# Attention layer: inverting the softmax denominators on 32 partitions, and subtracting the mean through the weights

## The reference

```python
Q, K, V = (split_heads(x_flat @ W + b) for W, b in ((Wq, bq), (Wk, bk), (Wv, bv)))   # 4 heads of 32
attn = softmax(einsum('bhnd,bhmd->bhnm', Q, K) * scale, axis=-1)
out = einsum('bhnm,bhmd->bhnd', attn, V).transpose(0, 2, 1, 3).reshape(B, H * W, C)
y = out @ Wo + bo + x_flat
mu = mean(y, axis=-1)                       # over the 128 channels
var = mean(square(y - mu), axis=-1)
y = (y - mu) / sqrt(var + 1e-5) * gamma + beta
```

## Time and profile before

| What | Value |
|---|---|
| median of three runs | 5654.49 us |
| the profiled execution | 5656.6 us, span 5654.8 us |
| PE, DVE busy | 5338.5 us (94%), 4949.7 us (88%) |
| POOL, ACT busy | 4692.7 us (83%), 3876.3 us (69%) |
| first exp tile of slot 0, last finish's z stored (first layer) | about 94 us to 3768 us |
| mean DMA rate | 97 GB/s |

### The profile page before, as it was taken

The page is one execution under the profiler, slowest core; times in us unless marked ns, Lnnn a source line. Parts: engine busy times, 40 slices in busy tenths (PEclk is TensorE's granted clock), DMA queues, the critical chain, the costliest instruction groups (busy, mean ns, idle before and its releaser), DMA issues. The chain is left out here.

```text
span 5654.8 us, 81519 instructions
## 1 busy us (share of the span) xinstructions
PE 5338.5 (94%) x25264; PEld 2432.7 (43%) x25264; DVE 4949.7 (88%) x7220; ACT 3876.3 (69%) x7513; POOL 4692.7 (83%) x3661
## 2 busy tenths in 40 slices
PE   7999999999999999999999999968888888888888
PEld 3444444444444444444444444423333333333333
DVE  6888888888888888888888888829999999999998
ACT  3666666666666766666666666657777777777776
POOL 4888887888888788888788888747888888888887
PEclk8999999999999999999999999989999999999999
DMA  4111122211111211112211010225555555555555
GB/s 139 36 53 50 37 61 71 60 55 38 46 49 64 79 39 53 45 40 62 64 54 33 18 32 21 67 84 196 186 190 188 188 187 189 186 188 190 186 188 174
DMA packets 337475, 549.14 MB, mean 97 GB/s; under 512 B 76016, under 2 KB 99568, under 8 KB 335600
## 3 DMA queue, kind: packets, MB, share of 16 engines
q1 hardware_dynamic: 327536, 526.62, 28.8%
q10 hardware_dynamic: 9504, 17.31, 1.1%
HBM read 415.10 MB, written 109.84 MB: 93 GB/s over the span
## 5 line engine op out<-in xcount | busy, mean ns | idle before, releaser
L649 DVE TENSOR_REDUCE mpart<-ps 128x1 f32<-128x512 f32 x4096 | 2539.1, 682 | 536.4 <-PE ps L406 535.8
L533 ACT ACTIVATE exps<-ps 128x512 f32<-128x512 f32 x4096 | 2146.8, 600 | 1139.8 <-PE ps L413 1114.1
L406 PE MATMUL ps<-k_st,q_ring 96*128 96x512 f32 x4096 | 1778.2, 435 | 20.2 <-DMA k_st<-qk_split 15.6
L413 PE MATMUL ps<-q_ring,k_st 98*128 98x512 f32 x4096 | 1621.5, 397 | 3.8 <-ACT exps L533 3.4
L1300 POOL TENSOR_TENSOR hc<-hh,c_rep 128x512 f32<-128x512 f32 x1024 | 1295.8, 1278 | 310.8 <-DVE hh L1269 291.8
L1269 DVE TENSOR_TENSOR_SCAN hh<-d_a,carry,ps 128x512 f32<-128x512 f32 x1024 | 1311.9, 1284 | 0.0
L622 POOL TENSOR_TENSOR held<-exps 128x512 f32<-128x512 f32 x768 | 987.7, 1311 | 359.9 <-ACT exps L533 359.9
L406 PEld LDWEIGHTS ps<-k_st,q_ring 96*128 96x128 f32 x4096 | 774.7, 189 | 1136.5 <-DVE mpart L649 685.2
L622 POOL TENSOR_TENSOR sums<-exps 128x512 f32<-128x512 f32 x896 | 1134.5, 1282 | 72.0 <-ACT exps L533 70.0
L424 PE MATMUL ps<-exps,v_ring 128*32 128x512 f32 x8192 | 1092.4, 605 | 0.0
L413 PEld LDWEIGHTS ps<-q_ring,k_st 98*128 98x128 f32 x4096 | 778.3, 190 | 139.7 <-ACT exps L533 18.0
(11 more groups left out here) (113 smaller groups left out, 3881.3 us busy)
## 6 DMA issues: line engine op xcount, KB each, us to landing
d_a<-dt_dram SPq DMA_DIRECT2D x1040, 256.0 KB
qk_split<-hilo SPq DMA_DIRECT2D x128, 256.0 KB, 2.3
out_dram<-out_sb SPq DMA_DIRECT2D x128, 256.0 KB, 2.0
heads_in<-out_dram SPq DMA_DIRECT2D x32, 1024.0 KB, 5.2
q_ring<-qk_split SPq DMA_DIRECT2D x384, 64.0 KB, 2.0
k_st<-qk_split SPq DMA_DIRECT2D x45, 512.0 KB, 7.4
dt_dram<-dt SPq DMA_DIRECT2D x33, 512.0 KB, 5.5
s_u<-lo_u ACTq DMA_DIRECT2D x66, 256.0 KB, 5.9
```

The lines of the kernel that those rows point to most:

```text
L406: nc.tensor.matmul(d_bank(("max", m, t)), q_ring[0:PARTS, m % 4, 128 * i:128 * i + 128], k_st[0:PARTS, g % 2, chunk(kc)], start=True, stop ...
L413: nc.tensor.matmul(a_bank(("exp", n, t)), k_st[0:SHIFT, n // NCH % 2, 128 * t:128 * t + 128], q_ring[0:SHIFT, n % 4, :], start=True, stop= ...
L533: nc.scalar.activation(exps[:, u % EXPS, CH * half:CH * half + CH], a_bank(("exp", n, t)), ACT.Exp, scale=SCALE).then_inc(a_done, 1)
L649: nc.vector.tensor_reduce(mpart[:, m % 2, t % 4, t // 4:t // 4 + 1], d_bank(("max", m, t)), AX.X, ALU.max).then_inc(d_done, 1)
```

## The change

Four things, all in the first layer.

- **Denominators.** The parts of each head (4 rows of 512) go to DRAM, cut into 8 pieces of 64 columns, and come back as 32 partitions (head, piece) by 4 by 64 (`load_den`). DVE sums the four and takes the reciprocal (`invert`, step 4). SP stores the 32 by 64 reciprocals, waits for that to land, and loads them with each head's row repeated on its 32 partitions into `recip` (`spread_rec`). The product `spread_den`, and Ln and Exp on ACT, are gone.
- **Mean.** Once, in slot 6, DVE subtracts from each row of Wo its mean over output channels, and from bo its mean (`centre_weights`), so that the projection's result has mean zero. The mean of x over channels comes from a column of 1/128 beside Wv: the V projection has 129 columns, its extra one goes through `mean_st` to DRAM (one more store a projection), and each finish loads it back repeated on 128 partitions (`mean_x`). DVE makes x + bo - mean in step 1 (`centre_x`); `centre` adds it to the projection. The product with 1/128 and `add_x` are gone.
- **V in two parts.** 4 times 129 columns do not fit in one bank, so V takes two entries of DVE's ring, of three and one blocks, with two DVE operations each.
- **Order.** The join moves from step 5 to 6, normalisation from 5 to 6, the output projection from 6 to 7.

Left out of the diff below: setup loads and declarations, the removed functions `spread_den`, `mean`, `reciprocal` and `add_x` with their calls, which stand in the listing above, and what only renames.

```diff
--- before.py
+++ after.py
                 if v == 6:
-                    add(d, ("value", p))
+                    add(d, ("value", p, 0))
+                    add(d, ("value", p, 1))
             if g is not None and v == 1:
                 add(a, ("var", g))
             if f is not None:
-                if v == 4:
-                    add(a, ("den", f))
+                if v == 7:
+                    add(d, ("wo", f))
                 if v == 6:
-                    add(d, ("wo", f))
-                if v == 7:
-                    add(d, ("mean", f))
-                if v == 5:
                     add(d, ("join", f))
...
     out_dram = nc.dram_tensor("out_dram", [2, HEADS, 128, L], F32, kind="Internal").ap()
+    den_dram = nc.dram_tensor("den_dram", [2, NCH, HEADS, 8, 4, CH // 8], F32, kind="Internal").ap()
+    rec_dram = nc.dram_tensor("rec_dram", [HEADS, CH], F32, kind="Internal").ap()
+    mean_dram = nc.dram_tensor("mean_dram", [NF, CH], F32, kind="Internal").ap()
...
+        den_in = sb("den_in", [32, 4, CH // 8])
+        den = sb("den", [32, CH // 8])
+        rec = sb("rec", [32, CH // 8])
+        mean_st = sb("mean_st", [128, 4])
+        mean_x = sb("mean_x", [128, CH])
...
-                    sp.wait_ge(d_done, d_at["value", p] + 1)
+                    sp.wait_ge(d_done, d_at["value", p, 1] + 1)
+                    sp.dma_start(mean_dram[p, :].rearrange("(q j) -> q j", j=4), mean_st[:, :]).then_inc(mean_stored, 16)
                     sp.dma_start(v_dram[b, :, :, 128 * c:128 * c + 128].rearrange("h p x -> p h x"),
                                  v_stage[:, :, :, :].rearrange("p h t d -> p h (t d)")).then_inc(v_stored, 16)
...
                 def store_den(n):
                     f = batch_of(n) * NCH + n % NCH
-                    row, half = den_rows(f)
-                    row += 4 * (n // NCH % HEADS)
                     sp.wait_ge(den_read, n + 1)
-                    if f >= NCH:
-                        sp.wait_ge(a_ready, a_at["den", f - NCH] + 1)
-                    sp.dma_start(denom[row:row + 4, half, :], den_parts[::D, n % 2, :]).then_inc(den_stored[n % 2], 16)
+                    if f >= 2 * NCH:
+                        sp.wait_ge(den_loaded, 16 * (f - 2 * NCH + 1))
+                    sp.dma_start(den_dram[batch_of(n) % 2, n % NCH, n // NCH % HEADS, :, :, :].rearrange("k q l -> q k l"),
+                                 den_parts[::D, n % 2, :].rearrange("q (k l) -> q k l", k=8)).then_inc(den_stored[n % 2], 16)
+
+                def load_den(f):
+                    sp.wait_ge(den_stored[f % 2], 16 * (last_slot(f) // 2 + 1))
+                    if f:
+                        sp.wait_ge(den_summed, f)
+                    sp.dma_start(den_in[:, :, :], den_dram[f // NCH % 2, f % NCH, :, :, :, :].rearrange("h k q l -> (h k) q l")
+                                 ).then_inc(den_loaded, 16)
+
+                def spread_rec(f):
+                    sp.wait_ge(rec_ready, f + 1)
+                    if f:
+                        sp.wait_ge(recip_ready, 16 * f)
+                        sp.wait_ge(d_done, d_at["join", f - 1] + 1)
+                    sp.dma_start(rec_dram.rearrange("h (k l) -> (h k) l", k=8), rec[:, :]).then_inc(rec_stored, 16)
+                    sp.wait_ge(rec_stored, 16 * f + 16)
+                    sp.dma_start(recip[:, :], rec_dram.rearrange("h (o l) -> h o l", o=1).to_broadcast([HEADS, D, CH])).then_inc(recip_ready, 16)
...
                         load_x(projection_at(n + 1))
                     if f is not None:
                         if f:
-                            sp.wait_ge(d_done, d_at["wo", f - 1] + 1)
+                            sp.wait_ge(x_ready, f)
                         sp.dma_start(x_f[:, :], x[f // NCH, :, chunk(f % NCH)]).then_inc(f_in, 16)
+                        sp.wait_ge(mean_stored, 16 * f + 16)
+                        sp.dma_start(mean_x[:, :], mean_dram[f, :].rearrange("(o l) -> o l", o=1).to_broadcast([128, CH])).then_inc(f_in, 16)
...
                     if 0 <= n + 1 < NS:
                         store_max(n + 1)
+                    if f is not None:
+                        load_den(f)
                     if g is not None:
                         store_z(g)
+                    if f is not None:
+                        spread_rec(f)
...
+                def project_v(p, part):
+
+                    key = "value", p, part
+                    d_room(key)
+                    for i, j in enumerate((range(3), (3,))[part]):
+                        ins = nc.tensor.matmul(d_bank(key)[:, (C + 1) * i:(C + 1) * i + C + 1], xc[:, p % 2, 128 * j:128 * j + 128],
+                                               wv[:, :], start=True, stop=True)
                     ins.then_inc(d_ready, 1)
...
                 def out_proj(f):
+                    if f == 0:
+                        pe.wait_ge(wo_ready, 2)
                     pe.wait_ge(d_done, d_at["join", f] + 1)
...
                             if v == 6:
-                                project_v(p)
+                                project_v(p, 0)
+                                project_v(p, 1)
...
                             variance(g)
...
+                        if f is not None and v == 7:
+                            out_proj(f)
...
-                        if f is not None and v == 5:
+                        if f is not None and v == 6:
                             join_heads(f)
...
-                    act.wait_ge(d_done, d_at["mean", f] + 1)
+                    act.wait_ge(d_done, d_at["wo", f] + 1)
...
+                def values(p, part):
+                    n, j = ((3, 0), (1, 3))[part]
+                    key = "value", p, part
+                    ready(key)
+                    if p and part == 0:
                         dve.wait_ge(v_stored, 16 * p)
+                        dve.wait_ge(mean_stored, 16 * p)
+                    bank = d_bank(key)[:, 0:n * (C + 1)].rearrange("p (t c) -> p t c", t=n)
+                    nc.vector.tensor_copy(mean_st[:, j:j + n].rearrange("p (t o) -> p t o", o=1), bank[:, :, C:C + 1])
                     nc.vector.tensor_tensor(
-                        v_stage[:, :, :, :].rearrange("p h t d -> p t h d"),
-                        d_bank(("value", p)).rearrange("p (t h d) -> p t h d", t=4, d=D),
-                        bv_sb[:, :].rearrange("p (o h d) -> p o h d", o=1, d=D).to_broadcast([128, 4, HEADS, D]), ALU.add
+                        v_stage[:, :, j:j + n, :].rearrange("p h t d -> p t h d"),
+                        bank[:, :, 0:C].rearrange("p t (h d) -> p t h d", d=D),
+                        bv_sb[:, :].rearrange("p (o h d) -> p o h d", o=1, d=D).to_broadcast([128, n, HEADS, D]), ALU.add
                     ).then_inc(d_done, 1)
+
+                def centre_weights():
+                    nc.vector.tensor_reduce(off[:, 0:1], w_sb[:, 3, :], AX.X, ALU.add).then_inc(off_ready, 1)
+                    nc.vector.tensor_reduce(off[:, 1:2], bo_sb[:, :], AX.X, ALU.add).then_inc(off_ready, 1)
+                    dve.wait_ge(off_ready, 2)
+                    nc.vector.tensor_scalar_mul(off[:, :], off[:, :], -1.0 / C).then_inc(off_ready, 1)
+                    dve.wait_ge(off_ready, 3)
+                    nc.vector.tensor_scalar(w_sb[:, 3, :], w_sb[:, 3, :], off[:, 0:1], None, ALU.add).then_inc(wo_ready, 1)
+                    nc.vector.tensor_tensor(bias[:, 2:3], bias[:, 2:3], off[:, 1:2], ALU.add).then_inc(wo_ready, 1)
+
+                def centre_x(f):
+                    dve.wait_ge(f_in, 32 * f + 32)
+                    if f == 0:
+                        dve.wait_ge(wo_ready, 2)
+                    else:
+                        dve.wait_ge(d_done, d_at["wo", f - 1] + 1)
+                    nc.vector.scalar_tensor_tensor(y_sb[:, :].rearrange("p (j q) -> p j q", j=4), x_f[:, :].rearrange("p (j q) -> p j q", j=4),
+                                                   bias[:, 2:3], mean_x[:, :].rearrange("p (q j) -> p j q", j=4), ALU.add, ALU.subtract
+                                                   ).then_inc(x_ready, 1)
+
+                def invert(f):
+                    dve.wait_ge(den_loaded, 16 * f + 16)
+                    if f:
+                        dve.wait_ge(rec_ready, f)
+                    nc.vector.tensor_reduce(den[:, :], den_in[:, :, :].rearrange("p q l -> p l q"), AX.X, ALU.add).then_inc(den_summed, 1)
+                    dve.wait_ge(den_summed, f + 1)
+                    if f:
+                        dve.wait_ge(rec_stored, 16 * f)
+                    nc.vector.reciprocal(rec[:, :], den[:, :]).then_inc(rec_ready, 1)
 
...
                     ready(("join", f))
-                    dve.wait_ge(recip_ready, f + 1)
+                    dve.wait_ge(recip_ready, 16 * f + 16)
                     nc.vector.tensor_tensor(normed[:, :], d_bank(("join", f)), recip[:, :], ALU.mult).then_inc(d_done, 1)
...
+                def centre(f):
                     ready(("wo", f))
...
```

(48 more changed lines are left out.)

37 lines of the change are left out of this document (6 added, 31 removed).

## The result

The changed kernel takes 5705.35 us (median of four runs, 5703.37 to 5709.52) where the kernel before takes 5652.84 us on the same chip (four runs). The ratio is 1.0093, with a 95% interval of 1.0075 to 1.011: slower by 0.9%, where a gain of 0.2% was forecast. 5705 us is also outside the range of 5630 to 5662 us.

The account below looks back on a forecast made before the run. VectorE was taken to bound plain slots, TensorE by little the finish slots. Terms -23.8 - 3.8 + 11.1 + 2.4 + 2.0 + 0.6 + 0.9 = -10.6 us gave a median of 5644 us, range 5630 to 5662.

Parts of the forecast that it names:

- finish slots: First layer, the 29 slots that carry finish work: each gains 0.82 us, from 31.41 to 30.6 us, -23.8 us in all.
- The path: Order along VectorE in a finish slot: no idle from step 2 to 7, next slot at 975.69 + I, not 977.43.
- The reciprocal: Step 4 of finish slots, VectorE, 64 columns: 0.56 us, the geometric middle of bounds 0.25 and 1.23 us.
- K's load: Slots 32, 64 and 96: the means queue behind the next head's K (1.5 MB), +11.1 us (0 to +14).
- rival 2: Slots 32, 64, 96: K's load does not hold the means; 11 us come off, 5633 us; chance 14%.
- Rival 1: Finish slots: TensorE stays the bound, each gains 2.1 us, -48 us in all, 5607 us; chance 6%.
- Rival 4: Finish slots: the reciprocal costs what ScalarE's pair does, 0.67 us more in 29 slots, +19, 5663 us; chance 8%.
- Rival 3: Step 6 of finish slots: normalisation waits for the late spread; beyond 6.5 us each microsecond costs 29 us; chance 12%.
- the tail: Last finish, nothing covering the DMAs: normalisation 4 us later, 3 us back from the mean's product and eviction, +0.9 us.
- The prelude: Eight slots at the start: one more SP store, beside landing waits, and two more VectorE operations each, +2.0 us.
- the last two slots: End of the first layer, no maximum tiles: two products of 1.1 us go, less the normalisation's wait, -3.8 us.
- The first step: Step 1 of finish slots: the moved two-operand pass with x costs 0.67 us, hidden in 1.14 us of VectorE idle.

## Why the prediction was wrong

**The step that failed** is in the finish slots: that the two-operand pass, moved to step 1, costs 0.67 us, which VectorE's 1.14 us of idle hides. The figure came from L692 (it stands in the earlier trace rows; the prediction names), whose first operand lay in PSUM. The moved operation has both in SBUF, one of them strided, beside a working GpSimd: 1.87 us from start to start. 0.7 us stuck out, and step 2 grew from 3.08 to 3.60. GpSimd's work beside VectorE had been put at nothing, without a reason. The pass to scaled, priced at no change, then ran into it too: 0.8 us more, and step 3 grew from 3.07 to 3.94. Both together make up nearly all of the 1.5 us a slot that leaving GpSimd idle gives back, where the whole error of a slot is 32.31 - 30.59 = 1.7. The last 0.2 us is the sum, sized at 0.41 and measured at 0.60 for its stride (0.398 without it). A row for a pass with both operands in SBUF stood in the trace of before: scaled, 813 ns, longer than the 692 and 688 of the passes over PSUM. That excess should have been asked about.

**The path was right, the sizes were not.** VectorE without idle from step 2 to 7, tiles of step 5 late, plain slots unchanged: all seen. The reciprocal was right (0.54 for 0.56 us), but with luck: 0.56 was the middle of two bounds, 0.25 and 1.23, neither of them near. The Trainium skill (VectorE: DVE Perf Modes, First, the fixed hardware budget), read as a pass eight times as long, gave an estimate of 0.68 us, the time of a tile of 512 columns; the row is nearer to that than to the 0.25 us of one pass, so the rule points the right way, though no run here shows the count of 8.

**K's load** held the means as forecast (12.2 for 11.1 us), and rival 2 fell: the wait is there, 10.6 us, three times, nowhere else. The sum is better than its parts: 4.3, 3.2 and 4.7 us for 4.4, 4.3 and 2.4.

**Rival 1** fell: no ordinary slot came near 29.3 us. **Rival 4** fell with the reciprocal's row. **Rival 3** has a part: the spread takes 1.36 us to the load's issue and, in the tail, 3805.41 - 3800.55 = 4.9 us to land, where 2.9 was read from a plain load of the same 256 KB. Store, wait and load come to 6.3 us, where 4.2 to 5.1 were forecast and 6.5 was the number from which it was to decide. So ordinary slots passed with a few tenths of a microsecond to spare in place of 1.4, and three of them waited 0.15 to 0.31 us. In slots 124 and 125 the waits are 1.2 and 0.8 us, about what these two slots lost beyond the others; there x and the means of the next finish are issued 0.6 us behind the spread's load. The load itself is slow: in an ordinary slot DMA moves 98 GB/s for it at a mean busy share of 0.26 (950 to 951 us), against 279 GB/s at 0.88 for x and the means (957.1 to 958.1 us). Its outermost dimension is the four heads; whether that is what holds it at a quarter was not tested. In the tail nothing covers it:

```profile
3797.98 0.59 DVE L718 TENSOR_REDUCE den<-den_in 32x64 f32<-32x256 f32 x1 [2.74 <-DMA den_in<-den_dram]
3798.61 0.54 DVE L722 RECIPROCAL rec<-den 32x64 f32<-32x64 f32 x1
3805.41 0.69 DVE L727 TENSOR_TENSOR normed<-ps,recip 128x512 f32<-128x512 f32 x1 [6.26 <-DMA recip<-rec_dram]
```

The tail is +5.0 us for +0.9: the spread is 1.3 us longer than the 5 forecast, and most of the rest is that the parts of the denominators land 13.7 us after the last exp, about 2.5 later than the forecast's times imply. **The prelude**, +6.5 for +2.0: the stores were taken as hidden beside waits for landings, and they are not. V in two parts was priced at 2.4 us in the slots and cost nothing there; the last two slots gained 1.5 more than said. The 2.3 us after the last z remain open; the other kernels show -0.7 to +2.0 us there, and none changes the second layer's code.

The first step doesn't explain the side alone. The changed kernel with GpSimd idle beside the two passes took 5664.64 us (one run), still 12 above the kernel before. Beyond the forecast stand there 0.2 us for the sum in 29 slots, about 4 us each in the prelude, in the tail and behind K's load, and 0.9 us in the first finish slot of each image.

## What to carry to other kernels

When an operation moves, price it with the operands it will have and the engines that will run beside it, not by its old row: whether an operand lies in PSUM or SBUF, the stride, and GpSimd's work made 0.74 us into 1.95, and an operation next to it, unchanged, went from 0.81 to 1.45. Where two rows of equal size differ in the trace (813 against 692 ns), find out why before the longer kind is put on the bounding engine. And look which slots are free of the work that a big load delays before moving it: all of K's loads moved two slots later gave 2 us, those of three slots alone 11.

## What was unexpected of the hardware

- A VectorE pass over two SBUF operands, 128 by 512, took 0.72 us beside an idle GpSimd and 1.63 beside a busy one; another, with 16 bytes between the elements of one operand, 1.12 and 1.95.
- Its cost is one of phase: the same unchanged instruction averaged 813, 1447 and 868 ns in three kernels, and 727 in the one in which GpSimd idles beside it.
- The sum of 256 elements on 32 partitions took 0.60 us with a stride of 256 bytes between the four values of one sum, 0.40 with neighbours.
- A broadcast load of 256 KB from 8 KB of DRAM took 4.9 us from its issue to the start of the product that waits for it, while the broadcast of one row of 2 KB to the same size landed in 3.6 (median). The first kept the DMA engines busy to a quarter.
- ScalarE's Ln and Exp on 32 by 64 took 0.26 us each and GpSimd's additions on 32 partitions 0.45 and 0.31, so together they are a little longer than VectorE's sum and reciprocal (0.60 and 0.54), but not on the engine that bounds the slot.
